# Layer 0 and layer 1: the engines' strip loops with four strips a turn in place of two

## Chip, cores and metric

The kernel runs on one core of a Trainium2 chip. The time is device microseconds (us) of one execution of the whole program; three runs of the kernel before took 21,091.03, 21,097.66 and 21,103.62 us. A core has TensorE (PE in the profile; PEld is its weight load), VectorE (DVE), ScalarE (ACT), GpSimd (POOL) and SyncE (SP). Each runs its own stream of instructions from memory, and they meet through semaphores. DMA queues carry data; among them are queues of the kind "instruction", which bring the engines their own programs.

## What is computed

Four images of 48 channels and 256 x 256 pixels go through six layers, each of them `x + layer(norm(x))`. The layers' kinds are in the name, `ccbcdd` being this program's letters; what the change touches are layer 0 and layer 1 (cut):

```
# layer 0
hidden = conv1x1(x, w_hidden);  qkv = depthwise3x3(hidden);  q, k, v = split(qkv, 3)
out = irfft2(rfft2(patches8x8(q)) * rfft2(patches8x8(k)))
normed = (out - mean_c(out)) / sqrt(var_c(out) + 1e-5) * gamma + beta
y = conv1x1(v * normed, w_out)
# layer 1
y = einsum(w_in, x);  y = irfft2(rfft2(patches8x8(y)) * fft_mask)
x1, x2 = split(depthwise3x3(y), 2);  y = einsum(w_out, gelu(x1) * x2)
```

Layer 2 samples an integral image of its input at four corners of a box for each pixel (a gather), and layer 3 is again a convolution, a gate and a patch transform.

## The kernel before

An image is worked in 32 strips of 8 rows. For each image in turn (`build`): layer 0 (for images 1 to 3 together with the box gather of the image before, `boxes`), then layer 1, the integral image, and the front of layer 2. The last box gather runs beside layer 3, which comes at the end for all images. So layer 0 and layer 1 run four times each, and each call has code of its own: the program holds four copies of either loop.

**Layer 0** (`layer0`, tag `a`) is a software pipeline with a step for every quarter strip of two rows, 128 steps an image. `pipeline` (L411) writes the steps of one engine: the first strip pair (8 steps) plainly, then a hardware loop over `u` (L421) with 8 steps a turn and 14 turns, then the last pair plainly and two steps that drain. PE, ACT and DVE each have their own loop of this shape. SP's loop over strip pairs (L486) and POOL's gather loop (L1828) are written apart. In a step PE makes the convolution for q and k of two rows (`conv_qk`, L530 and L533, into `p_qk`), the combination (L566), the convolution for v (L303 and L307, into `p_v`), the transforms of q and k (L547) and four transposes (L596). ACT begins a step with `gain` (L619), copies `p_qk` to `qk` (L614), takes two sums for the norm (L626, L633), and ends with `nrm` (L652) and `qh` (L661). DVE multiplies `t3` by `gain` (L701), and blends the gathered boxes in between (L1894, L1900). A loop's end therefore stands between L661 and L619 on ACT, and between L596 and L530 on PE.

**Layer 1** (`layer1`, tag `b`) is a pipeline with a step for every strip. Its `pipeline` (L822) has three plain steps, a loop with two steps a turn and 14 turns (L835), and five plain steps. A step has sixteen slots; PE's depthwise convolution is written as 16 small matmuls for each of 18 taps (L1010), so that a step of PE is some 1,600 instructions. A step begins on PE with `widen` (L966) and inverse transforms (L974), on ACT with the gelu of the strip before (L1129), on DVE with `weigh` (L1199) and `gates` (L1221). L1163 on ACT (the rows that strips share) runs once a step.

Semaphore targets are linear in the strip's number. Inside a loop they are computed from the loop's register, which costs an ALU instruction here and there.

Counted in the program as built, with matmuls and weight loads apart and register and wait instructions counted too, one turn of a loop is:

| loop | PE | ACT | DVE |
|---|---|---|---|
| layer 0, image 0 / images 1 to 3 | 1,045 / 1,081 | 323 | 202 / 222 |
| layer 1, image 0 / images 1 to 3 | 3,192 / 3,233 | 191 | 171 / 241 |
| layer 3, images 0 to 2 / image 3 | 2,342 / 2,260 | 181 | 378 to 380 / 238 |

Of the kernel before, what the change touches and what calls it, by code (L numbers as in the profile page):

```python
# [358 lines left out]
def layer0(env, src, dst, p, b, boxes=None, stats=None):  # L359
# [4 lines left out]
    U = S // 2  # L364
    C2, C6 = 2 * C, 6 * C
    with ExitStack() as ctx:
# [45 lines left out]
        def pipeline(eng, begin, step):  # L412

            n0 = b * (4 * S) + CREDIT
            begin(n0)
            for k in range(8):
                step(0, k, n0 + k, True, k >= 1, k >= 2, k >= 2 and k % 2 == 0)
            if U > 2:  # L420
                with eng.Fori(1, U - 1) as u:  # L421
                    for k in range(8):
                        step(u, k, n0 + u * 8 + k, True, True, True, k % 2 == 0)
            nl = n0 + 8 * U
            for k in range(8):
                step(U - 1, k, nl - 8 + k, True, True, True, k % 2 == 0)
            step(U, 8, nl, False, True, True, True)
            step(U, 9, nl + 1, False, False, True, False)
# [5 lines left out]
        with nc.Block() as block:  # L434
# [67 lines left out]
            def _(pe):  # L502
# [50 lines left out]
                def step(u, k, n, front, back, back2, turn_box):  # L553
# [35 lines left out]
                    if back:  # L589
# [5 lines left out]
                        for t in range(4):  # L595
                            m = pe.transpose(p_c[0:C2, 128 * t:128 * t + 128], nrm[:, t, :], env.c("ident"))  # L596
                            if beat and t == 0:
                                boxes.beat(m)
                        m.then_inc(turned_ready, 1)
                pipeline(pe, begin, step)  # L600

            @block.scalar
            def _(act):
# [5 lines left out]
                def step(u, k, n, front, back, back2, turn_box):  # L609
# [45 lines left out]
                    if front:  # L655
                        for h in range(2):
# [3 lines left out]
                            bank = p_f[0] if h == 0 else p_qk[0]  # L660
                            act.activation(qh[:, h, :, :].rearrange("p t c -> p (t c)"), bank[0:NPROD, 0:4 * C2], ACT.Copy).then_inc(qh_copied, 1)  # L661
                pipeline(act, lambda n0: None, step)

            @block.vector
            def _(dve):
# [29 lines left out]
                def step(u, k, n, front, back, back2, turn_box):  # L695
# [38 lines left out]
                    if front:  # L734
# [5 lines left out]
                        for h in range(2):  # L740
# [4 lines left out]
                            dve.tensor_tensor(prod[k % 2][:, h, :, :].rearrange("p t c -> p (t c)"), bank[0:NPROD, 0:4 * C2],  # L745
                                              qh[:, h, :, :].rearrange("p t c -> p (t c)"), ALU.mult).then_inc(prod_ready, 1)
                pipeline(dve, begin, step)


def layer1(env, src, dst, p, b, boxes=None):  # L750
# [6 lines left out]
    U = S // 2  # L757
# [23 lines left out]
    with ExitStack() as ctx:  # L781
# [43 lines left out]
        def pipeline(eng, begin, step):  # L825


            def half(u, k):
                return (U + u, k) if boxes else None
            n0 = b * S1 + 2  # L830
            begin(n0)
            step(n0, 0, True, False, False, False, None, True)
            step(n0 + 1, 1, True, True, False, False, half(0, 0), True)
            step(n0 + 2, 0, True, True, True, False, half(0, 1), True)
            with eng.Fori(0, U - 2) as u:  # L835
                step(n0 + u * 2 + 3, 1, True, True, True, True, half(u + 1, 0), True)
                step(n0 + u * 2 + 4, 0, True, True, True, True, half(u + 1, 1), True)
            step(n0 + S - 1, 1, True, True, True, True, half(U - 1, 0), True)
            step(n0 + S, 0, True, True, True, True, half(U - 1, 1), False)
            step(n0 + S + 1, 1, False, True, True, True, None, False)  # L840
            step(n0 + S + 2, 0, False, False, True, True, None, False)
            step(n0 + S + 3, 1, False, False, False, True, None, False)

        with nc.Block() as block:
# [86 lines left out]
            def _(pe):  # L931
# [91 lines left out]
                def step(n, par, front, mid, back, tail, half, more):  # L1023
                    m, o, l = n - 1, n - 2, n - 3
                    for t in range(NT):
# [55 lines left out]
                        if mid and t in CONV:  # L1081
                            taps(m, z[1 - par], *CONV[t], (2 if t in (3, 7, 10, 14) else 1) if half else 0)
                pipeline(pe, begin, step)

            @block.scalar
            def _(act):
# [50 lines left out]
                def step(n, par, front, mid, back, tail, half, more):  # L1137
                    m, o, l = n - 1, n - 2, n - 3
                    for t in range(NT):
# [29 lines left out]
                        if mid and t == 14:  # L1169
                            act.wait_ge(chain, (m + 1) * LINKS)  # L1170
                            act.wait_ge(y_ready, (m - 1) * NP)
                            act.activation(g_d[1 - par][HI], acc[0:64], ACT.Gelu).then_inc(gelu_ready, 1)
                pipeline(act, begin, step)

            @block.vector
            def _(dve):
# [46 lines left out]
                def step(n, par, front, mid, back, tail, half, more):  # L1223
                    m, o, l = n - 1, n - 2, n - 3
                    links = 0
                    for t in range(NT):
# [35 lines left out]
                        if mid and t == 15:  # L1262
                            dve.wait_ge(gelu_ready, m * 5 + 3)
                            dve.tensor_tensor(g_d[1 - par][HI], g_d[1 - par][HI], acc[HI], ALU.mult).then_inc(mul_ready, 1)
                pipeline(dve, begin, step)


# [1260 lines left out]
```

## Time and profile before

| | |
|---|---|
| median of three runs | 21,097.66 us |
| the profiled execution: its time / its span | 21,103.45 / 21,101.9 us |
| PE busy | 19,033.5 us (90% of the span) |
| DVE / ACT / POOL busy | 13,401.1 / 7,503.4 / 10,333.9 us |
| queue q8, instruction | 1,213 packets, 19.87 MB |
| queue q14, instruction | 570 packets, 4.67 MB |

The span runs from the first to the last instruction, 1.55 us less than the execution's own time. The four stretches of layer 0's loop lie near 376 to 1,736 us (image 0), 4,496 to 5,924, 8,733 to 10,170 and 12,986 to 14,324; those of layer 1's loop near 2,060 to 3,372, 6,245 to 7,600, 10,490 to 11,854 and 14,645 to 16,001. A wait that ends in "issue" is idle time in which the engine waited for nothing that the profile shows: no semaphore held it, it had no instruction to run. Branches and register instructions are not in the engines' rows.

### The profile page before, as it was taken

The page shows a single profiled execution, that of the slowest core. Times are in us where ns is not written, and L with a number is a line of the kernel's source. Part 1 is how long each engine was busy: PE and PEld are TensorE (multiplying, and loading weights), DVE is VectorE, ACT ScalarE, POOL GpSimd, SP SyncE. Part 2 cuts the span into 40 slices and gives each one's busy share as a digit, 9 for nine tenths or more (in the row PEclk, how much of TensorE's full clock was granted, in tenths as well). Part 3 has the DMA queues.
Part 4 walks back from the last instruction along what each step waited for, and adds up shares of the span by engine and source line. Part 5 has one row for each costly group of instructions (what it writes and reads, how often), then busy time and mean ns, then how long its engine had stood idle before and what let it go on. Part 6 is the DMA issues. An engine that isn't in the chain of part 4 may idle for free. (4 is left out here: it accounts for less than half of the span.)

```text
span 21101.9 us, 501412 instructions
## 1 busy us (share of the span) xinstructions
PE 19033.5 (90%) x172464; PEld 11794.6 (56%) x172464; DVE 13401.1 (64%) x22319; ACT 7503.4 (36%) x22720; POOL 10333.9 (49%) x8692
## 2 busy tenths in 40 slices
PE   6998998989989989899899898999998989898999
PEld 4665455456655554566555445665555456565666
DVE  4444445656667776666677766666777667777744
ACT  3554232145542221455422214663222122222222
POOL 0000000067767740677677406886774078787810
PEclk9999999999999999999999999999999999999999
DMA  3231112655533336455333364553434666666633
GB/s 92 68 70 45 35 36 84 140 112 113 113 99 111 110 119 145 109 112 113 99 110 111 112 151 111 121 121 100 111 110 126 134 146 150 149 149 146 147 88 78
DMA packets 932423, 2318.18 MB, mean 110 GB/s; under 512 B 276340, under 2 KB 528504, under 8 KB 844124
## 3 DMA queue, kind: packets, MB, share of 16 engines
q1 hardware_dynamic: 500560, 1364.68, 27.8%
q0 software_dynamic: 430080, 928.96, 16.7%
q8 instruction: 1213, 19.87, 0.4%
q14 instruction: 570, 4.67, 0.1%
HBM read 1915.53 MB, written 385.13 MB: 109 GB/s over the span
## 5 line engine op out<-in xcount | busy, mean ns | idle before, releaser
L1840 POOL DMA_INDIRECT e_got<-table,e_idx x6144 | 7479.2, 1217 | 2580.1 <-issue 1603.5
L1856 POOL DMA_INDIRECT e_got<-table,e_idx x2048 | 2553.1, 1247 | 691.6 <-issue 501.7
L1010 PE MATMUL b_p_conv<-b_z,b_diag 32*32 32x512 f32 x76032 | 2807.1, 599 | 3.3 <-issue 3.3
L530 PE MATMUL a_p_qk<-a_wst,a_stack 125*128 125x192 f32 x12288 | 2466.8, 337 | 230.9 <-ACT a_qh L661 214.0
L530 PEld LDWEIGHTS a_p_qk<-a_wst,a_stack 125*128 125x128 f32 x12288 | 2025.8, 191 | 670.5 <-issue 367.5
L1112 ACT ACTIVATE b_z<-b_p_z 128x256 f32<-128x256 f32 x2112 | 846.5, 401 | 4026.9 <-PE b_p_z L974 3608.2
L1894 DVE TENSOR_TENSOR e_got<-e_got,e_wt 128x1536 f32<-128x1536 f32 x1024 | 1778.6, 1752 | 684.9 <-DMA e_got<-table,e_idx 682.3
L1199 DVE TENSOR_TENSOR b_ym<-b_p_in,b_mask 128x512 f32<-128x512 f32 x1056 | 729.4, 691 | 1807.8 <-PE b_p_in L966 1807.6
L974 PEld LDWEIGHTS b_p_z<-const,b_ym 128*128 128x128 f32 x8448 | 1165.3, 198 | 1215.5 <-issue 713.3
L974 PE MATMUL b_p_z<-const,b_ym 128*128 128x128 f32 x8448 | 1541.1, 307 | 100.1 <-ACT b_z L1112 93.9
L2140 PE MATMUL d_p_v<-d_xs,d_ws 125*128 125x512 f32 x4608 | 1388.2, 449 | 64.0 <-issue 60.4
L1900 DVE TENSOR_TENSOR e_got<-e_got 128x1536 f32<-128x1536 f32 (+1 forms) x1024 | 1386.6, 1354 | 23.4
L303 PE MATMUL a_p_v<-a_xs,a_ws 125*96 125x512 f32 x4608 | 1363.1, 440 | 0.0
L1341 POOL DMA_DIRECT2D i_x<-planes x256 | 132.2, 516 | 2477.7 <-issue 1864.1
L1010 PEld LDWEIGHTS b_p_conv<-b_z,b_diag 32*32 32x32 f32 x76032 | 861.2, 103 | 732.2 <-issue 439.1
L2140 PEld LDWEIGHTS d_p_v<-d_xs,d_ws 125*128 125x128 f32 x4608 | 884.1, 201 | 341.2 <-issue 74.0
L303 PEld LDWEIGHTS a_p_v<-a_xs,a_ws 125*96 125x96 f32 x4608 | 747.9, 162 | 541.4 <-issue 284.9
L614 ACT ACTIVATE a_qk<-a_p_qk 128x384 f32<-128x384 f32 x1024 | 502.8, 491 | 1502.4 <-PE a_p_qk L533 1315.9
L966 PE MATMUL b_p_in<-b_w,b_xf 64*128 64x288 f32 x4224 | 847.8, 477 | 191.5 <-issue 172.4
L533 PE MATMUL a_p_qk<-a_wrs,a_rest 66*128 66x192 f32 x4096 | 1009.0, 327 | 0.0
L926 POOL MEMSET b_x<- 113x2064 f32 x4 | 7.3, 1818 | 2026.8 <-POOLq L243 2026.8
L547 PE MATMUL a_p_f<-a_qk,const 64*94 64x384 f32 x2048 | 821.7, 523 | 174.0 <-ACT a_qk L614 174.0
(291 smaller groups left out, 35444.6 us busy)
## 6 DMA issues: line engine op xcount, KB each, us to landing
e_got<-table,e_idx POOLq DMA_INDIRECT x8192
b_x<-planes SPq DMA_DIRECT2D x264, 395.1 KB
a_stack<-in_xp SPq DMA_DIRECT2D x256, 387.0 KB
c_stack<-planes SPq DMA_DIRECT2D x256, 387.0 KB
d_stack<-planes SPq DMA_DIRECT2D x512, 193.5 KB
table<-i_acc SPq DMA_DIRECT2D x256, 384.0 KB, 2.3
b_xr<-planes SPq DMA_DIRECT2D x264, 197.5 KB
planes<-b_out SPq DMA_DIRECT2D x264, 197.5 KB
```

Source lines behind the costliest of these rows:

```text
L303: mm = pe.matmul(out, ws[i][:, dx, lo:hi], xs[j][:, r0:r0 + QROWS, dx:dx + W], start=(dx == i == j == 0), stop=False)
L530: m = pe.matmul(dst_, st[:, row, dx + 128 * t:dx + 128 * t + 128], wst[:, dx, 0:2 * C2], start=(dx == 0), stop=False)
L533: m = pe.matmul(dst_, rt[:, row, 128 * t:128 * t + 128], wrs[:, 0:2 * C2], start=False, stop=True)
L966: pe.matmul(p_in[:, h, 0:NC], xf[k % 2][64 * h:64 * h + 64, :], w[64 * h:64 * h + 64, :], start=True, stop=True).then_inc(in_ready, 1)
L974: mm = pe.matmul(p_z[:, 128 * g:128 * g + 128], ym[k // 2 % 2][:, k % 2, 128 * g:128 * g + 128], env.c("idft"), start=True, stop=True)
L1010: mm = pe.matmul(p_conv[q // 2 * 2 + r % 2][BLK * c:BLK * (c + 1), :], diag[g][BLK * r:BLK * (r + 1), k, :], zs[BLK * r:BLK * (r + 1), g, ...
L1112: act.activation(zs[:, :, 2:2 + SROWS, 1 + 16 * k:17 + 16 * k], p_z[:, 0:NA].rearrange("p (g y x) -> p g y x", y=SROWS, x=16), ACT.Copy).t ...
L1840: pool.indirect_dma_start(out=self.got[q][:, t, c * REC:(c + 1) * REC], out_offset=None, in_=self.flat, in_offset=bass.IndirectOffsetOnAxi ...
L1856: pool.indirect_dma_start(out=self.got[q][:, t, c * REC:(c + 1) * REC], out_offset=None, in_=self.flat, in_offset=bass.IndirectOffsetOnAxi ...
L1894: dve.tensor_tensor(part, part, self.wt[i][:, at:at + 32].unsqueeze(2).broadcast_to([128, 32, C]), ALU.mult).then_inc(self.halved, 1)
L1900: dve.tensor_tensor(got[:, :, 0:half], got[:, :, 0:half], got[:, :, half:2 * half], ALU.add).then_inc(self.halved, 1)
L2140: mm = pe.matmul(out, ws[i][:, dx, lo:lo + 128], part(xs[j][:, :, dx:dx + W], side), start=(dx == k == 0), stop=False)
```

## The change

The loops of `pipeline` in layer 0 and layer 1 take twice the steps a turn and half the turns: 16 quarter-strip steps in place of 8, and four strips in place of two, seven turns each in place of fourteen. The plain steps ahead and behind are the same, and so are the steps themselves, their order and their semaphore targets, which are now computed from `v`. The loops of SP and POOL and those of the other layers are not touched.

```
-                with eng.Fori(1, U - 1) as u:
-                    for k in range(8):
-                        step(u, k, n0 + u * 8 + k, True, True, True, k % 2 == 0)
+                with eng.Fori(0, (U - 2) // 2) as v:
+                    for j in range(2):
+                        for k in range(8):
+                            step(v * 2 + (j + 1), k, n0 + v * 16 + (8 * j + k + 8), True, True, True, k % 2 == 0)
...
-            with eng.Fori(0, U - 2) as u:
-                step(n0 + u * 2 + 3, 1, True, True, True, True, half(u + 1, 0), True)
-                step(n0 + u * 2 + 4, 0, True, True, True, True, half(u + 1, 1), True)
+            with eng.Fori(0, (U - 2) // 2) as v:
+                for j in range(2):
+                    for k in range(2):
+                        step(n0 + v * 4 + (2 * j + k + 3), 1 - k, True, True, True, True, half(v * 2 + (j + 1), k), True)
```

In the program as built, a turn is then:

| loop | PE | ACT | DVE |
|---|---|---|---|
| layer 0, image 0 / images 1 to 3 | 2,088 / 2,160 | 643 | 399 / 438 |
| layer 1, image 0 / images 1 to 3 | 6,380 / 6,459 | 377 | 337 / 477 |

On ACT in layer 0 the eighth step of a turn was followed by the loop's branch, which goes back to the loop's first instruction; what stands behind it in the program is the code after the loop:

```order
L652 ACTIVATE a_nrm<-a_p_o,a_shift,a_rs 128x96 x4
L659 REGISTER_ALU
L661 ACTIVATE a_qh<-a_p_f 94x384
L661 ACTIVATE a_qh<-a_p_qk 94x384
L421 REGISTER_ALU
L421 COMPARE_AND_BRANCH
L619 ACTIVATE a_gain<-a_p_c,a_beta,a_gamma 96x512
```

Now the ninth step follows the eighth without a branch (line numbers are one higher):

```order
L653 ACTIVATE a_nrm<-a_p_o,a_shift,a_rs 128x96 x4
L660 REGISTER_ALU
L662 ACTIVATE a_qh<-a_p_f 94x384
L662 ACTIVATE a_qh<-a_p_qk 94x384
L620 ACTIVATE a_gain<-a_p_c,a_beta,a_gamma 96x512
L612 ISA
L615 ACTIVATE a_qk<-a_p_qk 128x384
```

The same pair of a register instruction and a branch now stands behind the sixteenth step. PE and DVE read alike, and in layer 1 the branch moves from behind each second strip to behind each fourth.

## Rows read from the trace of the kernel before

**Rows 1.** Waits that ended in "issue": total us, times, longest us.
```profile
PE b_p_in L966 <- issue: 172.4, 56, 4.1
ACT a_gain L619 <- issue: 160.9, 39, 4.9
ACT a_qk L614 <- issue: 156.2, 26, 8.5
ACT a_junk L626 <- issue: 93.0, 13, 7.7
...
DVE d_xs L321 <- issue: 22.5, 5, 6.2
```

**Rows 2.** DMA packets of layer 0's loop, image 1: queue, kind, packets, MB.
```profile
q14 instruction: 65, 0.53, 0.1%
```

**Rows 3.** The same of image 3's loop, all its queues.
```profile
q1 hardware_dynamic: 25670, 79.04, 30.2%
q0 software_dynamic: 39886, 81.73, 24.1%
```

**Rows 4.** The same of layer 1's loop, image 0; of a layer-3 turn, image 3.
```profile
q8 instruction: 182, 2.98, 1.0%
...
q8 instruction: 11, 0.18, 0.5%
```

**Rows 5.** Line L619, once a step: count, ns, first and last start (us).
```profile
L619 ACT ACTIVATE a_gain<-a_p_c,a_beta,a_gamma x6: 773/774/775, 409.4 to 472.5; 96x512 f32<-96x512 f32 x6
L619 ACT ACTIVATE a_gain<-a_p_c,a_beta,a_gamma x96: 772/774/777, 383.2 to 1617.6; 96x512 f32<-96x512 f32 x96
L619 ACT ACTIVATE a_gain<-a_p_c,a_beta,a_gamma x96: 772/773/776, 4503.4 to 5803.0; 96x512 f32<-96x512 f32 x96
L619 ACT ACTIVATE a_gain<-a_p_c,a_beta,a_gamma x96: 772/773/776, 8739.7 to 10047.1; 96x512 f32<-96x512 f32 x96
L619 ACT ACTIVATE a_gain<-a_p_c,a_beta,a_gamma x96: 772/773/776, 12988.5 to 14209.6; 96x512 f32<-96x512 f32 x96
```

**Rows 6.** Timeline at a loop end of layer 0, image 1: start, us, engine [idle before].
```profile
4717.63 1.24 PE L530 MATMUL a_p_qk<-a_wst,a_stack 125*128 125x192 f32 x6 [0.45 <-ACT a_qh L661]
...
4730.33 0.20 ACT L626 ACTIVATION_READ_ACCUMULATOR a_junk<-a_p_o 128x1 f32 x1 [6.94 <-issue]
...
4733.17 0.94 PE L547 MATMUL a_p_f<-a_qk,const 64*94 64x384 f32 x1 [4.97 <-ACT a_qk L614]
```

**Rows 7.** Line L1163, once a step of layer 1, as in rows 5.
```profile
L1163 ACT ACTIVATE b_z<-b_z x2: 1075/1075/1075, 3382.2 to 3428.3; 128x1032 f32<-128x1032 f32 x2
L1163 ACT ACTIVATE b_z<-b_z x26: 1074/1074/1076, 2125.2 to 3336.1; 128x1032 f32<-128x1032 f32 x26
L1163 ACT ACTIVATE b_z<-b_z x2: 1074/1074/1074, 6210.3 to 6257.9; 128x1032 f32<-128x1032 f32 x2
L1163 ACT ACTIVATE b_z<-b_z x26: 1074/1074/1077, 6310.6 to 7562.4; 128x1032 f32<-128x1032 f32 x26
L1163 ACT ACTIVATE b_z<-b_z x26: 1073/1074/1077, 10556.1 to 11816.6; 128x1032 f32<-128x1032 f32 x26
L1163 ACT ACTIVATE b_z<-b_z x26: 1073/1075/1077, 14710.3 to 15963.4; 128x1032 f32<-128x1032 f32 x26
```

**Rows 8.** Timeline at a loop end of layer 1, image 0.
```profile
2594.06 1.08 ACT L1129 ACTIVATE b_ga<-b_p_conv 128x512 f32<-128x512 f32 x2 [0.92 <-PE b_p_conv L1010]
2596.90 1.33 PE L966 MATMUL b_p_in<-b_w,b_xf 64*128 64x288 f32 x4 [3.11 <-issue]
...
2598.40 0.69 DVE L1199 TENSOR_TENSOR b_ym<-b_p_in,b_mask 128x512 f32<-128x512 f32 x1 [6.55 <-PE b_p_in L966]
...
2599.14 1.28 DVE L1221 TENSOR_TENSOR b_gate<-b_p_conv,b_ga 128x512 f32<-128x512 f32 x2
```

**Rows 9.** Windows around it: busy us (instructions) by engine, granted clock, DMA share, GB/s.
```profile
2575.00:2592.00 17.00, 17.00 (x315) 8.23 (x313) 6.87 (x15) 4.40 (x12) 0.00 (x0) 1.00 0.14 50
2597.00:2602.00 5.00, 5.00 (x12) 2.69 (x13) 2.02 (x4) 0.40 (x1) 0.00 (x0) 0.50 0.02 3
```

## Prediction

> **What bounds the kernel, and what a loop's end costs.** I read four views: the waits that end in "issue", the packets of the instruction queues, one line that runs once a step over each image's loop, and the timeline at a loop's end. PE sets the pace of both stages (17.00 us busy in a stretch of 17.00 [rows 9]), so what counts is what a loop's end does to PE. I call the jump from a loop's last instruction to its first a seam. A loop of 14 turns has 13, and the four images have 52 in each layer.
>
> In layer 0 it is ACT that pays. Its first instruction of a turn, L619, came late for want of an instruction 39 times, 4.1 us each: 13 seams of three images [rows 1]. A second stall of 6.0 to 7.2 us follows a few instructions later (26 + 13 times, on L614 or L626 [rows 1]). Image 1's loop fetched 65 packets from an instruction queue, five a seam [rows 2]; image 3's loop runs the same code and fetched none [rows 3]. ACT's loop of 323 instructions is thus sometimes kept whole and sometimes not, by where it happens to begin in memory. That makes image 3 a measurement of the same layer without seams: 95 steps took 1,221.1 us there, against 1,299.6 in image 1 and 1,307.4 in image 2 [rows 5]. Over the 11 whole seams in those stretches that is 78.5 / 11 = **7.1** and 86.3 / 11 = **7.9** us a seam. Image 0 has no boxes; its undisturbed step is 63.1 / 5 = 12.62 us, so 1,234.4 - 95 x 12.62 = 35.5, **3.2** us a seam [rows 5].
>
> In layer 1 it is PE that pays: 172.4 / 56 = 3.1 us before L966 [rows 1], 14 packets a seam (182 / 13 [rows 4]), since each turn of 3,192 instructions is fetched anew. Then PE runs at half its clock for a while (granted 0.50 behind the seam, 1.00 ahead of it, that is 1.2 in place of 2.4 GHz [rows 9]). An undisturbed step is 46.1 us in image 0 and 47.6 in image 1, for which two steps ahead of the loop stand [rows 7]. The 25 steps from the first to the last row hold 12 seams: (1,210.9 - 25 x 46.1) / 12 = **4.9**, and with 47.6 (1,251.8, 1,260.5 and 1,253.1 - 1,190) / 12 = **5.2, 5.9, 5.3** us.
>
> So seams cost today: layer 0, 13 x (3.2 + 7.1 + 7.9 + 0) = **237 us**; layer 1, 13 x (4.9 + 5.2 + 5.9 + 5.3) = **277 us**.
>
> **The change part by part.**
>
> Fewer seams: seven turns have 6, so 24 in place of 52 in each layer. No step, wait or order inside a turn changes, and the fewer branches and register instructions lie under PE's work.
>
> Layer 1, PE: still too long to be kept, the same price a seam. 6 x 21.3 = 128 us remain.
>
> Layer 1, ACT and DVE: their loops grow from 191 to 377 and from 171 or 241 to 337 or 477 instructions. Whether such a length is kept is seen from both sides: 323 both was and was not [rows 2, 3], 378 to 380 of DVE in layer 3 paid a stall of 22.5 / 5 = 4.5 us at its first instruction [rows 1]. I take DVE to miss in images 1 to 3 and leave ACT open. The cover is PE's own stall: DVE's L1199 waited 6.55 us, for PE and not for itself, and ACT's L1129 could start 2.84 us ahead of PE's L966 and is wanted by L1221 only at 2,599.14 [rows 8]: a delay of 4.1 us would move its end from 2,595.1 to 2,599.2, just there. I take 0.5 us a seam, with 0 and 3 as ends (ACT's second stall is not covered). Sum: 128 + 24 x 0.5 = **140 us**, so layer 1 gains 277 - 140 = **137 us** (range 277 - 128 - 72 = 77 to 149).
>
> Layer 0, ACT: 643 instructions, twice what misses in three images, so it misses in all four; image 3 now pays as images 1 and 2, 7.5 us. 6 x (3.2 + 7.1 + 7.9 + 7.5) = 154 us.
>
> Layer 0, PE: a new miss. A turn of 1,081 fetched nothing from q8 [rows 3], one of 2,260 in layer 3 fetched 11 packets [rows 4]. The new 2,088 and 2,160 lie close to the upper one, so I take it that they are fetched, at layer 1's 3.1 us of stall. In images with boxes this falls into a hole: PE's first matmul behind the seam waits for ACT's L661 anyhow, and later PE stands 4.97 us for ACT's L614 [rows 6]. What PE does late is taken from that hole. Image 0 has a smaller one (3.2 us of loss), so I add 1 us there. DVE's loop of 399 or 438 misses too, 4.5 us, while its next work, L701, waits for ACT's L619 (itself late by 4.1). I take 1 us a seam on every image for all this (0 and 3 as ends; below nothing is excluded, as no engine gets anything earlier). Sum: 154 + 24 x 1 = **178 us**, so layer 0 gains 237 - 178 = **59 us** (11 to 83; to 109 if image 3's ACT pays only 3.2).
>
> Fetching in the body: PE's loop in layer 0 now draws some 9 packets in 205 us. Layer 1 draws 14 in 97 us, and of the 56 waits before L966 that ended in "issue" 52 are its seams [rows 1]. I take nothing.
>
> Here the Trainium skill says something sharper. "Runtime: NRT & Kernel Launch", section "Instruction fetch mechanics", gives PE room for 2,048 instructions and the other engines for 512, filled in sequence, and says that a taken branch out of the window waits for a fetch. By its sizes PE's loop in layer 0, which fits today, falls out, which speaks against this change and is what the sum has taken from layer 3's row. By the same sizes ACT's loop of 323 fits wherever it begins and the new one of 643 does not; rows 2 and 3 contradict the first half. What would follow from the page there is rival E.
>
> Sum: 137 + 59 = **196 us**. The profiled execution took 21,103.45 us, which gives 20,907; it lies 5.8 us above the median of the three runs, so against the median **20,902 us**.
>
> **The rivals.**
>
> A. The forecast: 20,902 us. Its ends: all extras zero and image 3 cheap, 149 + 109 = 258 us, 20,840; extras of 3 us everywhere, 77 + 11 = 88 us, 21,010.
>
> B. PE's loop in layer 0 stays in place and no seam is dearer than today: 237 - 154 + 277 - 128 = 232 us, 20,866. For it: 2,088 and 2,160 are less than 2,260. Against it: the nearness.
>
> C. The stalls of one seam do not overlap but follow each other, because the three engines now ask for code at once while SP's loads and the gather use the same DMA engines. Then layer 0's seam takes 3.1 (PE) + 4.5 (DVE) = 7.6 us more: 6 x (25.7 + 30.4) = 337; layer 1's 4.1 (ACT) + 4.5 (DVE) = 8.6 more: 6 x (21.3 + 34.4) = 334. Together 671 against 514 us today: slower by 157, 21,255. For it: ACT's second stall is longer than the first [rows 1, 6]. Against it: the seams are nearly one point in time on all engines, and only the last to be ready counts. It decides from 24 x 2 seams dearer by (514 - 282) / 48 = 4.8 us each.
>
> D. PE starves inside the longer layer-0 body: at 0.75 us for each of some 9 packets x 28 turns the gain is gone, 21,098. Layer 1 shows no such stall.
>
> E. ACT's lost time in layer 0 is not the seam's and stays (237 us), and the longer loops of PE, ACT and DVE bring seams of their own on top, 178 us, against the 137 of layer 1: slower by 41, 21,139. The Trainium skill's sizes ("Runtime: NRT & Kernel Launch", "Instruction fetch mechanics") would have it so. Against it: image 3 loses nothing with the same code, and fetches nothing [rows 3, 5].
>
> **How the numbers follow.** A 0.78, B 0.10, C 0.05, D 0.04, E 0.03. The predicted time is A's. The range is A's ends, 20,840 to 21,010; it takes in B and leaves out C, D, E and a little of A, some 0.15. A measurement of this kernel tells about 0.2%, 42 us, from no change. Faster by more than that: A and B but for a little, 0.87; within: D, E and the rest of A, 0.08; slower: C, 0.05.
>
> **What would show it.** The waits for "issue" before L966 in layer 1 fall from 52 to about 24 with the same 3 to 4 us each; those of ACT at L619 from 39 to 24, now in image 3 as well. The q8 queue, absent from layer 0's loop, brings 9 or 10 packets a turn there; if it stays absent, B holds. In image 3's layer 0 the 95 steps get longer, by 5 or 6 seams of some 7.5 us, while those of images 1 and 2 get shorter by about as much. If seams in either layer take over 4.8 us more than today, C holds and the forecast is wrong.

## The result, and the profile after

The changed kernel takes **20,808.31 us** (median of 4 runs, 20,799.02 to 20,813.51) against 21,094.35 us beside it: ratio 0.9863, 95% interval 0.9848 to 0.9878. That is 286 us less, where 196 were forecast; the time lies 32 us below the range of 20,840 to 21,010. The direction was right, the size was not. Between the two profiled executions the difference is 297.5 us (spans 21,101.9 and 20,804.4 us).

The waits of the changed kernel that end in "issue" (total us, times, longest us) answer to [rows 1]; lines are one or two higher:

```profile
DVE a_t L702 <- issue: 97.4, 19, 6.5
ACT a_mu L631 <- issue: 86.5, 18, 6.6
PE b_p_in L968 <- issue: 79.2, 28, 3.9
ACT a_gain L620 <- issue: 73.4, 24, 4.1
...
DVE e_got L1896 <- issue: 49.2, 6, 8.6
PE a_p_qk L531 <- issue: 48.2, 25, 5.7
```

PE's stalls in layer 1 went from 56 to 28, ACT's at the head of a layer-0 turn from 39 to 24. New are PE's at L531, 25 of 1.9 us (before there was a single one): PE's layer-0 loop is fetched now. The packets of image 3's loop say the same, where [rows 3] had none (queue, kind, packets, MB, share of the 16 engines):

```profile
q8 instruction: 69, 1.13, 0.4%
q14 instruction: 76, 0.62, 0.2%
```

ACT's line that runs once a step of layer 0, over the whole of each image (first and last start, us):

```profile
L620 ACT ACTIVATE a_gain<-a_p_c,a_beta,a_gamma x128: 772/772/776, 198.0 to 1802.2; 96x512 f32<-96x512 f32 x128
L620 ACT ACTIVATE a_gain<-a_p_c,a_beta,a_gamma x128: 765/772/777, 4236.1 to 5933.0; 96x512 f32<-96x512 f32 x128
L620 ACT ACTIVATE a_gain<-a_p_c,a_beta,a_gamma x128: 765/772/775, 8411.1 to 10066.0; 96x512 f32<-96x512 f32 x128
L620 ACT ACTIVATE a_gain<-a_p_c,a_beta,a_gamma x128: 765/772/776, 12547.5 to 14196.6; 96x512 f32<-96x512 f32 x128
```

These are 1,604.2, 1,696.9, 1,654.9 and 1,649.1 us; the same line of the kernel before took 1,641.4, 1,721.8, 1,728.9 and 1,630.4. So layer 0 gained 117 us, twice the forecast's 59, and unevenly: 37, 25, 74 and -19.

And the line of layer 1 of [rows 7], over the same 26 steps:

```profile
L1165 ACT ACTIVATE b_z<-b_z x26: 1073/1076/1078, 2077.5 to 3260.3; 128x1032 f32<-128x1032 f32 x26
L1165 ACT ACTIVATE b_z<-b_z x26: 1072/1075/1077, 6204.9 to 7425.1; 128x1032 f32<-128x1032 f32 x26
L1165 ACT ACTIVATE b_z<-b_z x26: 1073/1075/1077, 10336.7 to 11561.5; 128x1032 f32<-128x1032 f32 x26
L1165 ACT ACTIVATE b_z<-b_z x26: 1074/1075/1077, 14468.5 to 15685.4; 128x1032 f32<-128x1032 f32 x26
```

With the forecast's steps of 46.1 and 47.6 us, (1,182.8 - 1,152.5) / 6 = 5.1 us a seam, and 5.0, 5.8 and 4.5: what the kernel before paid. Over all 32 rows of the line layer 1 gained 150 us. Some 30 us more lie outside both layers' loops, 17 of them in layer 3.

So the question for the runs is layer 0: a seam there costs 1.3, 11.2, 3.7 and 3.3 us in images 0 to 3 (worked out below), where the forecast had 4.2, 8.1, 8.9 and 8.5.

### The profile page after: what moved, and what is told of

Its sections match the earlier page's. It is cut to its first block and busy times, and to the rows that moved or that the text cites. A ratio compares the mean times of both kernels' runs of the same rounds, so it can differ in the third digit from the quotient of the medians.

```text
span 20804.4 us, 500656 instructions
## 1 busy us (share of the span) xinstructions
PE 18912.8 (91%) x172464; PEld 11734.2 (56%) x172464; DVE 13400.9 (64%) x22319; ACT 7497.1 (36%) x22720; POOL 10324.5 (50%) x8692
## 5 line engine op out<-in xcount | busy, mean ns | idle before, releaser
L531 PE MATMUL a_p_qk<-a_wst,a_stack 125*128 125x192 f32 x12288 | 2463.9, 337 | 273.0 <-ACT a_qh L662 212.3
L531 PEld LDWEIGHTS a_p_qk<-a_wst,a_stack 125*128 125x128 f32 x12288 | 2023.2, 191 | 709.0 <-issue 438.6
L723 DVE SCALAR_TENSOR_TENSOR a_out<-a_p_y,a_bo,a_out 49x512 f32<-49x512 f32 x512 | 377.4, 737 | 917.0 <-PE a_p_y L582 917.0
```

The source lines that it names most:

```text
L531: m = pe.matmul(dst_, st[:, row, dx + 128 * t:dx + 128 * t + 128], wst[:, dx, 0:2 * C2], start=(dx == 0), stop=False)
```

## The theory, and its rival

Two timelines of the changed kernel at a seam show where the difference lies: image 1, then image 2 (start, us, engine, in brackets the idle time before and what ended it).

```profile
4740.81 1.24 PE L531 MATMUL a_p_qk<-a_wst,a_stack 125*128 125x192 f32 x6 [1.91 <-issue]
4742.64 0.77 ACT L620 ACTIVATE a_gain<-a_p_c,a_beta,a_gamma 96x512 f32<-96x512 f32 x1 [3.35 <-issue]
4750.06 0.21 ACT L631 ACTIVATE a_mu<-a_total 128x4 f32<-128x4 f32 x1 [4.48 <-issue]
4753.38 3.43 DVE L1896 TENSOR_TENSOR e_got<-e_got,e_wt 128x1536 f32<-128x1536 f32 x2 [8.38 <-issue]
4759.22 1.40 ACT L653 ACTIVATE a_nrm<-a_p_o,a_shift,a_rs 128x96 f32<-128x96 f32 x4 [5.93 <-DVE a_shift L730]
4760.67 1.09 PE L597 MATMUL a_p_c<-const,a_nrm 128*96 128x128 f32 x4 [6.92 <-ACT a_nrm L653]
```

```profile
8698.31 1.24 PE L531 MATMUL a_p_qk<-a_wst,a_stack 125*128 125x192 f32 x6 [1.53 <-issue]
8699.87 0.77 ACT L620 ACTIVATE a_gain<-a_p_c,a_beta,a_gamma 96x512 f32<-96x512 f32 x1 [2.69 <-issue]
8703.42 0.69 DVE L702 TENSOR_TENSOR a_t<-a_p_v,a_gain 96x512 f32<-96x512 f32 x1 [5.58 <-issue]
8704.03 3.42 DVE L1896 TENSOR_TENSOR e_got<-e_got,e_wt 128x1536 f32<-128x1536 f32 x2
8707.43 0.21 ACT L631 ACTIVATE a_mu<-a_total 128x4 f32<-128x4 f32 x1 [4.35 <-issue]
```

In image 1 DVE runs four or five instructions, stands 8.4 us for its next packet, and hands the delay on: ACT's norm waits 5.9 us for DVE, PE 6.9 us for ACT. In image 2 DVE has its second stall nowhere near.

A packet of q14 is 8,192 bytes (4.67 MB / 570). The Trainium skill, "Runtime: NRT & Kernel Launch", section "Instruction fetch mechanics", counts 256 instructions to 16 KiB, so by an estimate from its figure such a packet is 128 instructions. The runs below agree, as the second stalls fall where this count puts them.

**Theory T.** The program of ACT and DVE comes in packets of 128 instructions with fixed borders. A loop of ACT or DVE that lies in three packets is kept; one that lies in four is fetched anew at each seam. Then the first packet ends the first stall, and the second comes several us later. What a seam costs depends on the *room*: the instructions from the loop's start to the end of its first packet, which are all that the engine can do until the second comes. The borders were fitted to which of ACT's loops in the kernel before are kept. Its rooms in layer 0 are then 25, 10, 4 (fetched) and 126 (kept); in the changed kernel 25, 16, 16, 16 on ACT and about 22, 4, 101, 70 on DVE.

**Rival P.** Each image has a price of its own, by its boxes and transfers, as the forecast took it.

## Experiments: one layer at a time

Layer 0's loops alone (the first hunk of the change):

> Layer 0's loops with four strips a turn, layer 1's as before. Theory T (what a seam costs depends on where the loop begins in the packets of 128 instructions that bring the programs of ACT and DVE: few instructions left in the first packet make a dear seam): the instructions left in the first packet are now 25, 74, 4 and 62 on ACT and 22, 42, 119 and 68 on DVE for images 0 to 3, so image 1 becomes cheap and image 2 dear; 6 x (1.4 + 3 + 6 + 3) = 80 us of seams in place of 237, about 20,940 us. Rival P (each image has a price of its own whatever the position, as the prediction had it): with the prices measured in the changed kernel (1.4, 11.1, 4.3, 3.1 a seam) 120 us remain, 20,977 us, with image 1 the dear one; with the prediction's own terms 178 us, 21,035 us.

Measured: 20,945.47 us (ratio 0.9925, 0.9908 to 0.9941). T's total of 20,940 and its order of images held: with the undisturbed lengths from the next section, a seam costs 2.0, 3.0, 5.1 and 2.7 us. Image 1, dear in the changed kernel, is cheap; image 2 is the dear one.

Layer 1's loops alone (the second hunk):

> Layer 1's loops with four strips a turn, layer 0's as before. Theory T: layer 1 gains about 150 us, and its longer code moves the layer-0 loops behind it, so that ACT's loop of 323 instructions now lies in three packets in images 1 and 3 (80 instructions left in the first) and in four in images 0 and 2 (25 and 16 left): image 1 loses its seams too, no stall of ACT at its loop's end there. 41 + 0 + about 85 + 0 us of seams in layer 0 in place of 237: 20,840 us in all. Rival P (a price for each image, whatever the position): layer 0 as before, 20,945 us.

Measured: 20,825.74 us (0.9872, 0.9855 to 0.9888), within 14 us of T and 119 us below P. Though nothing of layer 0 is edited, image 1 has no stall of ACT at its seams any more (1,639.5 us, of which 9.5 at other steps that I can't explain); image 3 has none, as before (1,630.9), and image 2 (room 16) still has. The two halves alone gain 152 and 272 us; together they gain 286. The parts don't add up because either moves the code of the other.

## Experiments: the room

Thirty instructions, once, in the kernel before:

```
+                for _ in range([30, 0, 0, 0][b]):
+                    act.sem_inc(turn, 1)
                 pipeline(act, lambda n0: None, step)
```

> The kernel before with 30 instructions more on ACT (semaphore increments that nobody waits for), once, ahead of layer 0 of image 0. Theory T: ACT's loop of 323 instructions then begins with 123, 108, 102 and 96 instructions left in its first packet, so it lies in three packets in all four images and is kept; no instruction packet and no stall at layer 0's seams, the 237 us go, 20,860 us. Rival P (what sets the loss is the image: its boxes, its transfers): no change, 21,095 us.

Measured: 20,861.37 us (0.9887, 0.987 to 0.9903). Thirty increments take 233 us off, T's 237 almost to the unit. Layer 0's line in that kernel, images 0 to 3:

```profile
L619 ACT ACTIVATE a_gain<-a_p_c,a_beta,a_gamma x128: 772/772/776, 203.9 to 1800.2; 96x512 f32<-96x512 f32 x128
L619 ACT ACTIVATE a_gain<-a_p_c,a_beta,a_gamma x128: 772/772/775, 4268.5 to 5898.5; 96x512 f32<-96x512 f32 x128
L619 ACT ACTIVATE a_gain<-a_p_c,a_beta,a_gamma x128: 772/772/775, 8416.1 to 10048.9; 96x512 f32<-96x512 f32 x128
L619 ACT ACTIVATE a_gain<-a_p_c,a_beta,a_gamma x128: 772/772/775, 12576.7 to 14206.0; 96x512 f32<-96x512 f32 x128
```

1,596.4, 1,630.0, 1,632.8 and 1,629.3 us: layer 0 without seams, the base for all prices here (a kernel's length less this, by its seams). Each length is of one profiled execution; where no seam costs anything, an image's length differs by up to 2.5 us between the kernels below, 0.4 us a seam of six, so smaller differences of prices tell nothing. The kernel before thus paid 45.0 / 13 = 3.5, 91.8 / 13 = 7.1, 96.1 / 13 = 7.4 and 0.1 us, as the forecast had read it. Queue q14 brought 375 packets in place of 570: 195 fewer, five for each of 39 seams.

The other way, less room in image 3 and other rooms elsewhere (93 increments ahead of image 0, 12 ahead of image 2):

```
+                for _ in range([93, 0, 12, 0][b]):
+                    act.sem_inc(turn, 1)
                 pipeline(act, lambda n0: None, step)
```

> The kernel before with 93 instructions more on ACT ahead of layer 0 of image 0 and 12 more ahead of image 2, so that ACT's loop begins with 60, 45, 27 and 21 instructions left in its first packet (25, 10, 4 and 126 in the kernel before) and lies in four packets in every image. Theory T (position sets the price): the loop is fetched in all four images, image 3 too, and the price falls with the room: image 0 about 1.5 us a seam (3.5 before), image 1 about 3 (7.1 before), image 2 about 5 (7.4 before), image 3 about 6 (0 before); 13 x 15.5 = 200 us in place of 237, 21,060 us. Rival P (each missing image has one price, about 7 us with boxes): 13 x (3.5 + 3 x 7.2) = 326 us, 21,185 us. Rival N (image 3 has no seams whatever the position): image 3 unchanged.

Measured: 20,998.06 us (0.9957, 0.9943 to 0.9971). P and N fall: q14 has 637 packets, 262 more than with all kept (260 are five for each of 52 seams), so ACT is fetched in all four images, image 3 too, and still the kernel is faster than before. Borders every 256 instructions, a loop being kept in two such blocks, fall as well: images 0 to 2 would have had rooms of 188, 173 and 155 here and been kept.

```profile
L619 ACT ACTIVATE a_gain<-a_p_c,a_beta,a_gamma x128: 772/772/776, 204.5 to 1800.9; 96x512 f32<-96x512 f32 x128
L619 ACT ACTIVATE a_gain<-a_p_c,a_beta,a_gamma x128: 772/772/777, 4263.5 to 5905.1; 96x512 f32<-96x512 f32 x128
L619 ACT ACTIVATE a_gain<-a_p_c,a_beta,a_gamma x128: 772/772/775, 8422.8 to 10107.9; 96x512 f32<-96x512 f32 x128
L619 ACT ACTIVATE a_gain<-a_p_c,a_beta,a_gamma x128: 772/772/775, 12634.7 to 14332.7; 96x512 f32<-96x512 f32 x128
```

Prices 0, 0.9, 4.0 and 5.3 us at rooms of 60, 45, 27 and 21: T's order, but 133 us in all where I had set 200; large rooms are cheaper than I thought. The two stalls of a seam in image 3 of this kernel:

```profile
13365.68 0.77 ACT L619 ACTIVATE a_gain<-a_p_c,a_beta,a_gamma 96x512 f32<-96x512 f32 x1 [4.14 <-issue]
13374.53 0.34 ACT L633 ACTIVATE a_junk<-a_p_o,a_mu 128x96 f32<-128x96 f32 x1 [5.77 <-issue]
```

The second comes behind the 21st instruction, as counted; in image 2 of the run with layer 1 alone it came behind the 16th. In the images with boxes it ends some 13.5 us behind the branch whatever the room (some 12 in image 0), so the room decides only how much ACT has done by then. The first stall of 4 us alone costs under 1 us. All prices with ACT alone missing in an image with boxes:

| room | kept | 74, 62 | 45 | 27 | 21 | 16 | 10 | 4 |
|---|---|---|---|---|---|---|---|---|
| us a seam | 0 | 0.7, 0.9 | 0.9 | 4.0 | 5.3 | 6.2 | 7.1 | 7.4, 7.1 |

Eight instructions on DVE in the changed kernel:

```
+                for _ in range([0, 8, 0, 0][b]):
+                    dve.sem_inc(turn, 1)
                 pipeline(dve, begin, step)
```

> The changed kernel with 8 instructions more on DVE, once, ahead of layer 0 of image 1. Theory T: DVE's loop of 438 instructions there begins with 125 instructions left in its first packet in place of 4 or 5, its second stall (8 to 9 us) goes, and image 1's loop loses about 26 us in place of 67: 41 us less than the changed kernel, 20,767 us. Images 2 and 3 stay within 10 us. Rival P: no change against the changed kernel, 20,808 us.

Measured: 20,780.77 us (0.9849, 0.9832 to 0.9865 against the kernel before). Image 1's line:

```profile
L620 ACT ACTIVATE a_gain<-a_p_c,a_beta,a_gamma x128: 766/773/777, 4239.6 to 5887.8; 96x512 f32<-96x512 f32 x128
```

1,648.1 us in place of 1,696.9: a seam there costs 3.0 us in place of 11.2. DVE's second stall is gone from that image. Its layer 0 gave 49 us; the whole only 28, where T had 41, as layer 3 and the program's start were 14 and 7 us longer in this profile.

## Experiments: which engine's miss costs what

`pipeline` of layer 0 got a parameter, so that each engine's loop can have two or four strips a turn on its own; layer 1 as before. PE alone (with the 30 increments of above, so ACT is kept), ACT alone, ACT and PE, ACT and DVE:

```
-        def pipeline(eng, begin, step):
+        def pipeline(eng, begin, step, pairs=1):
...
-                pipeline(pe, begin, step)
+                pipeline(pe, begin, step, 2)
```

> Layer 0 alone: PE's loop four strips a turn; ACT's and DVE's two strips a turn, with the 30 instructions ahead on ACT that keep its loop whole (as in e3). So of layer 0's loops only PE's is fetched anew. The same kernel without PE's longer loop took 20,861 us. Theory T (ACT sets the price, PE's stall of about 1.7 to 2.5 us is partly made up): 1 to 2 us a seam, 24 to 48 us more, 20,885 to 20,910 us. Rival Q (PE's own stall is all of the 3 us that the changed kernel pays where ACT has room): 3 us a seam, 72 us more, 20,933 us.

> Layer 0 alone: ACT's loop four strips a turn, PE's and DVE's two. ACT's loop begins where it does in the run with all of layer 0 changed (25, 74, 4 and 62 instructions left), and of the three engines only ACT misses. Theory T (ACT's first packets set the price, whatever the others do): image 1 and 3 about 3 us a seam, image 2 5.6 us as there, 80 us of seams in all, 20,940 us. Rival S (a seam is cheaper when PE and DVE miss with ACT, since the same room on ACT, 4, cost 7.4 us with ACT alone in the kernel before): image 2 pays 7.4 us, 47 us in six seams in place of 33.

> Layer 0 alone: the loops of ACT and PE four strips a turn, DVE's two. ACT begins with 25, 74, 4 and 62 instructions left in its first packet, as with ACT alone (3.3, 1.0, 7.1 and 1.0 us a seam) and as with all three (2.0, 3.0, 5.5 and 2.7). Theory V (it is DVE's fetch beside it that brings ACT's second packet sooner): image 2 pays 7 to 8 us a seam, images 1 and 3 2 to 3, as PE's own 1.7 is added. Theory W (it is PE's stall that makes image 2 cheaper): image 2 pays about 5.5 us.

> Layer 0 alone: the loops of ACT and DVE four strips a turn, PE's two. DVE begins with 22, 42, 119 and 68 instructions left. Theory V (DVE's fetch brings ACT's second packet sooner): image 2 pays about 5 us a seam, images 1 and 3 about 1 to 2. Theory W (PE's stall makes it cheaper): image 2 pays 7 to 8 us.

Measured: 20,928.54 us (0.9927, 0.991 to 0.9943), 20,929.11 (0.9926, 0.9909 to 0.9942), 20,965.20 (0.9935, 0.9916 to 0.9955) and 20,954.46 (0.993, 0.9911 to 0.995). By image, us a seam:

| missing | image 0 | image 1 | image 2 | image 3 |
|---|---|---|---|---|
| room on ACT (all but the first row) | 25 | 74 | 4 | 62 |
| PE | 1.6 | 1.8 | 1.2 | 1.2 |
| ACT | 3.3 | 0.7 | 7.1 | 0.9 |
| ACT and PE | 2.1 | 2.7 | 6.5 | 2.4 |
| ACT and DVE | 2.7 | 3.0 | 6.9 | 3.9 |
| all three | 2.0 | 3.0 | 5.1 | 2.7 |

PE's own price is T's 1 to 2 us. The total, 67 us above the kernel without PE's longer loop, is nearer to Q's, but only 34 of them lie in layer 0. Another 28 lie in layer 1 of image 3, whose loop isn't edited but stands elsewhere in PE's program (1,571.8 us over the 32 rows, 1,543.8 without PE's longer loop); that the place is what costs it there is argued. Where ACT has much room, images 1 and 3, the prices of ACT and PE nearly add (0.7 + 1.8 and 0.9 + 1.2 against 2.7 and 2.4). Where it has little, image 2, more misses make the seam *cheaper*, so S held against T there. Neither V nor W did: PE takes 0.6 us off, DVE alone nothing that can be told (0.2), and both together 2.0. The second stall of ACT in image 2 ends 13.4 us behind its branch with ACT alone, 13.2 with DVE, 12.4 with PE, 11.8 with all. Part of PE's share shows in the traces: SP waits for PE's convolution, and with PE missing as well its first load of `a_stack` was issued 2.2 us behind ACT's branch in place of 1.5 (means of image 2), and ACT's first instruction came 3.9 us behind it in place of 4.7. The rest is open.

T's room thus sets the price of a seam where ACT misses alone. With all three missing, and DVE not short of room, the seams with boxes cost 3.0 and 2.7 us at rooms of 74 and 62 on ACT, 2.9 to 3.7 at 16 (the changed kernel with and without the eight instructions on DVE), and 5.1 at 4.

## Experiments: why the second packet is late

The DMA share at a seam of image 1 in the kernel before (windows; busy us and instructions of PE, PEld, DVE, ACT, POOL, then granted clock, DMA share, GB/s):

```profile
4717.00:4721.00 4.00, 3.55 (x22) 2.78 (x20) 1.02 (x2) 0.58 (x2) 3.08 (x4) 1.00 1.08 155
4721.00:4725.00 4.00, 4.00 (x25) 3.40 (x23) 2.24 (x2) 1.52 (x5) 3.08 (x4) 1.00 1.02 150
4725.00:4729.00 4.00, 3.20 (x13) 1.79 (x11) 3.72 (x5) 0.00 (x0) 3.56 (x2) 1.00 0.99 211
4729.00:4733.00 4.00, 0.00 (x0) 0.00 (x0) 0.00 (x0) 2.61 (x16) 0.95 (x1) 1.00 0.97 218
4733.00:4737.00 4.00, 3.63 (x12) 1.55 (x12) 2.62 (x6) 3.38 (x11) 0.95 (x1) 0.58 0.15 50
```

For 16 us behind the seam the DMA engines are full (a share near 1). The largest transfers issued in that stretch are SP's (KB each):

```profile
a_stack<-in_xp SPq DMA_DIRECT2D x2, 387.0 KB
a_out<-in_xp SPq DMA_DIRECT2D x1, 387.0 KB
a_stack<-in_xp SPq DMA_DIRECT2D x1, 217.7 KB
```

They are transfers for the next strips, due at a strip's end, just where the loop's branch stands. ACT's loop was therefore begun two steps later, in the middle of a strip, with the same small rooms:

```
+            for k in range(late):
+                step(1, k, n0 + 8 + k, True, True, True, k % 2 == 0)
...
-                with eng.Fori(1, U - 1) as u:
-                    for k in range(8):
+                with eng.Fori(1, U - 1 - (late > 0)) as u:
+                    for k in range(late, 8 + late):
...
-                pipeline(act, lambda n0: None, step)
+                for _ in range([52, 80, 80, 62][b]):
+                    act.sem_inc(turn, 1)
+                pipeline(act, lambda n0: None, step, 2)
```

> The kernel before, with ACT's layer-0 loop begun two steps later (steps 2 to 7 of a strip pair and 0 and 1 of the next, 13 turns, 12 seams) and 52, 80, 80 and 62 instructions ahead, so that it begins with 25, 10, 4 and 16 instructions left in its first packet: 25, 10 and 4 as in the kernel before for images 0 to 2, and 16 as in image 2 of the run with layer 1 alone. What is new is the place of the seam: two steps behind the point at which SP's loads of the next strips keep the DMA engines full (share 0.97 to 1.08 for 16 us behind a seam of image 1 in the kernel before, 0.2 to 0.3 two steps later). Theory B (the second packet waits for those loads): it comes soon behind the first, the second stall shrinks to under 3 us, and the price falls to 1 to 2.5 us: 12 x 6 = 72 us of seams in place of 237, about 20,930 us. Theory F (the engine asks for its second packet about 9 us after the first whatever the DMA engines do): prices as at the same room before, 3.5, 7.1, 7.4 and 6.4 us: 12 x 24.4 = 293 us, about 21,150 us.

Measured: 20,874.59 us (0.9899, 0.9882 to 0.9916): B, and more than B; F falls. The lengths are 1,602.4, 1,635.3, 1,632.3 and 1,632.3 us, so 12 seams cost 0.5, 0.4, 0 and 0.3 us each at rooms of 25, 10, 4 and 16. ACT is fetched as before (q14: 626 packets, 251 above the kept kernel's 375), yet it stands less: 3.2 us in the mean at the first instruction of a turn (48 times, image 0 up to 6.3), and the second stall is short. DMA share and stalls at such a seam of image 2, room 4:

```profile
8744.00:8748.00 4.00, 3.55 (x22) 2.97 (x20) 1.02 (x2) 1.30 (x3) 3.09 (x4) 1.00 0.49 137
8748.00:8752.00 4.00, 4.00 (x26) 3.33 (x26) 3.63 (x3) 2.22 (x13) 3.70 (x2) 1.00 0.37 101
```

```profile
8747.56 0.77 ACT L627 ACTIVATE a_gain<-a_p_c,a_beta,a_gamma 96x512 f32<-96x512 f32 x1 [2.39 <-issue]
8750.05 0.49 ACT L622 ACTIVATE a_qk<-a_p_qk 128x384 f32<-128x384 f32 x1 [1.72 <-issue]
```

The second stall is 1.7 us; with ACT alone missing at the strip's end and the same room it was 8.1:

```profile
9578.46 0.77 ACT L624 ACTIVATE a_gain<-a_p_c,a_beta,a_gamma 96x512 f32<-96x512 f32 x1 [4.24 <-issue]
9587.37 0.49 ACT L619 ACTIVATE a_qk<-a_p_qk 128x384 f32<-128x384 f32 x1 [8.14 <-issue]
```

The packets' own records in the traces say it directly. In the kernel before, ACT's second packet began 8.9, 9.5 and 9.3 us behind the first (means over the seams of images 0 to 2); here it began 2.4, 2.6, 2.4 and 2.4 us behind it. Image 0, beside which no gather runs, is as late as the others, so the gather isn't needed for it. That the packet waits behind SP's transfers fits all this, but no run moved those transfers themselves.

The same with all three engines of the changed kernel (cut; the loop from step 18 on, six turns, with instructions ahead on ACT and DVE that leave them as little room as in the changed kernel):

```
+                for g in range(8, 18):
+                    step(g // 8, g % 8, n0 + g, True, True, True, g % 2 == 0)
+                with eng.Fori(0, (U - 4) // 2) as v:
+                    for g in range(18, 34):
+                        step(v * 2 + g // 8, g % 8, n0 + v * 16 + g, True, True, True, g % 2 == 0)
```

> The changed kernel with layer 0's loops of PE, ACT and DVE all begun later, two steps into a strip (six turns of 16 steps, five seams an image), and with instructions ahead on ACT (4, 32, 32, 32) and DVE (82, 83, 67, 67), so that they begin with as little room as in the changed kernel: 25, 16, 16, 16 left on ACT, and about 22, 5, 102, 72 on DVE. Theory B (what makes a layer-0 seam dear is that second packets wait behind SP's loads, on DVE too): all seams cost 1 to 2 us, image 1's too, 20 x 1.5 = 30 us in place of 117, about 20,720 us. Rival R (DVE's second packet in image 1 is late for another reason): image 1 keeps about 9 us a seam, 70 to 80 us of seams, about 20,765 us.

Measured: 20,799.91 us (0.9863, 0.9847 to 0.988), no gain that can be told from the changed kernel, where B expected some 90 us. By image the lengths of 1,617.3, 1,648.5, 1,656.2 and 1,649.6 us are 4.2, 3.7, 4.7 and 4.1 us for each of five seams. Image 1 fell from 11.2 to 3.7, so DVE's late packet there went with the place too, and R falls. But B missed as well: the other images did not get cheaper, and 83 us of seams remain in layer 0 where 30 were expected. PE's stall there is 59.6 / 20 = 3.0 us, longer than the changed kernel's 1.9; that it sets these prices is argued:

```profile
ACT b_ga L1138 <- issue: 82.3, 24, 4.9
ACT a_gain L623 <- issue: 68.6, 20, 6.1
PE a_p_qk L534 <- issue: 59.6, 20, 4.5
```

The first of these rows is new: the added instructions put ACT's layer-1 loop of 377 into four packets, and it misses at all 24 seams of layer 1. Over the four images layer 1 is 21 us longer than in the changed kernel, 0.9 us a seam. That is not ACT's price alone: the edit moves PE's loops too, beside which layer 1 of image 3 became 28 us longer in the run with PE alone, and image 0 got no longer (1,454.1 us over the 32 rows, 1,456.3 in the changed kernel) though ACT misses there as well.

## Experiments: a version that beats both

If a kept loop has no seams, layer 0 needs no longer turns, only ACT's room. Layer 0 as before with increments ahead, and layer 1 without a loop (28 strips written out, first with 30 ahead in image 0, then 55, 50, 59 and 59 in the four images and layer 3 written out as well) or with 14 strips in each of two turns (55, 15, 36 and 30 ahead):

```
-            with eng.Fori(0, U - 2) as u:
+            for u in range(U - 2):
...
-                with eng.Fori(0, TURNS) as v:
+                for v in range(TURNS):
```

```
+            M = 7
+            with eng.Fori(0, (U - 2) // M) as v:
+                for j in range(M):
+                    for k in range(2):
+                        step(n0 + v * (2 * M) + (2 * j + k + 3), 1 - k, True, True, True, True, half(v * M + (j + 1), k), True)
```

> A version that should beat both: layer 0's loops as before (two strips a turn, kept by PE and DVE), with the 30 instructions ahead on ACT that keep its loop too; layer 1 without a loop (28 strips written out on PE, ACT and DVE). Theory T: no seams in either layer; 237 + 277 = 514 us less than before, 20,580 us, if straight code is fetched ahead in time. Rival D (PE, ACT or DVE starve in straight code, as a packet is fetched anew for each strip): layer 1 gains nothing, about 20,860 us.

> Layer 1 without a loop, layer 0 as before. In the first such run the code of layer 1 had moved ACT's layer-0 loop to 45 and about 35 instructions left in images 1 and 3, and these paid 1.0 and 3.1 us a seam, 52 us. Here 55, 50, 59 and 59 instructions ahead bring it to about 98 left in every image. Layer 3 is written out too (four turns of six strips, where DVE stalled 4 to 6 us at the seams of three images). Theory T: the 52 us go, 20,615 us, and layer 3 gives 0 to 40 us: 20,575 to 20,615 us.

> Layer 0 as before, with instructions ahead on ACT (55, 15, 36 and 30 for images 0 to 3), so that its loop begins with 98 to 104 instructions left in its first packet in every image and is kept. Layer 1: 14 strips in each of two turns, so one seam an image. Theory T: layer 0 has no seams (237 us less), layer 1 keeps 21 of 277 us: 493 us less than before, 20,600 us; if straight code in layer 1 costs the 0.5 us a step that it cost without a loop, 42 us more, 20,642 us.

Measured: 20,667.72 us (0.9799, 0.9782 to 0.9815), 20,606.25 (0.9765, 0.9749 to 0.9781) and **20,585.95** (0.9755, 0.9738 to 0.9771). The last beats the changed kernel by 222 us and the kernel before, run beside it, by 515. Of PE's waits for an instruction before its first matmul of a layer-1 step 8 are left:

```profile
PE b_p_in L970 <- issue: 15.8, 8, 4.0
```

The first of the three fell short since the longer layer 1 had moved ACT's layer-0 loops again: images 1 and 3 had rooms of about 45 and 35 and lost 12.5 and 40 us. With the rooms set anew that went. Written out, a step of layer 1 in images 1 to 3 takes 48.0 us, in a loop 47.5, so that in layer 1 one seam beats none, by 14 us in all; the cause of that half us is not known.

## Why the forecast was wrong

- **The seam as the unit, and that it is a fetch**: right. Prices read as 3.2, 7.1, 7.9 and 0 us were 3.5, 7.1, 7.4 and 0.1 against a layer 0 without seams.
- **Layer 1, 137 us**: right in its main term, 150 measured. The price of a seam stayed (20.4 us for the four images, 21.3 before [rows 7]), and 24 remain. The 0.5 us for ACT and DVE, 12 us in all, was not paid: ACT's loop of 377 instructions lies in three packets and is kept, and DVE shows no wait for an instruction in layer 1. Where ACT's loop was not kept, the seams were 0.9 us dearer, with PE's code moved as well.
- **Layer 0, ACT, 154 us**: this step failed in its price. That "it misses in all four" was right, and so was image 3's loss. But 6 x (3.2 + 7.1 + 7.9 + 7.5) carried prices of one layout over to another, and the change itself altered the rooms, to 25, 16, 16 and 16. At the prices of ACT missing alone (3.3 at 25 in image 0, 6.2 at 16 with boxes) I estimate 6 x (3.3 + 3 x 6.2) = 131 us.
- **Layer 0, PE and DVE, 1 us a seam, "below nothing is excluded, as no engine gets anything earlier"**: this step failed, and by more. PE misses, as taken (the Trainium skill's "Runtime: NRT & Kernel Launch", "Instruction fetch mechanics", gives it 2,048 instructions; 2,088 and 2,160 were fetched, 1,081 not), but stalls 1.9 us, not 3.1, and costs 1.2 to 1.8 alone. With ACT short of room, the misses of PE and DVE took time off the seam in place of adding to it, and ACT did get its instructions earlier: the changed kernel with eight instructions ahead on DVE pays 6 x (1.3 + 3.0 + 2.9 + 3.4) = 64 us where ACT alone would pay the estimated 131. Why it is that much stays open. Against it stands DVE's miss in image 1, 8 us a seam by a room of four, outside the 0 to 3 that I allowed. Together: 178 us forecast, 6 x (1.3 + 11.2 + 3.7 + 3.3) = 117 measured. That image 1's dear seam made up for part of the miss was luck: without it the kernel took 20,780.77 us, further still from the forecast.
- **The rest**: some 30 us outside the two loops were not forecast. Layer 3's code is the same but stands elsewhere; thirteen other kernels with the same layer 3 took 4,193 to 4,213 us for it, against 4,216 before and 4,199 after. I leave the cause open.
- **Rival B** fell (q8's packets in image 3's loop), **D** too (no stall of that size in the body). **E** fell: ACT's loss in layer 0 was the seams', since it went with them. The same section of the Trainium skill gives ACT 512 instructions, by which size alone a loop of 323 fits wherever it begins, as E took it; but it puts them in two lines of 256, by which the place matters. Here 30 instructions ahead decided whether the loop was fetched. **C** named SP's loads on the same DMA engines, which the seam in mid-strip bears out as far as the place goes, and had the wrong consequence: the stalls of three engines overlap, and with little room on ACT they are together cheaper than ACT's alone (5.1 against 7.1), with much room dearer by 2 us.
- Image 3 [rows 2, 3] was read well: kept "by where it happens to begin in memory". The forecast knew this and still used a price that hangs on the same position as if it were a constant. The range was too narrow for a term that the layout moves between 0 and 11 us a seam.

## What to carry to other kernels

A loop that is fetched anew at its branch, on one engine alone, costs what this engine can't do until the *second* packet lands, so look at where its branch stands against the big loads and how far behind its start a packet ends, before making it longer. Where several engines are fetched anew at one point, don't add their prices: measure them together. Any edit to one stage moves the code of all later ones: count where each loop begins after the edit, and don't carry a stall's size over from the old layout. Where a loop nearly fits, a few dozen idle instructions ahead of it can be worth more than half the turns, and the branch can be moved to a quiet place in the work.

## What the hardware showed

- A loop of 323 instructions on ACT was kept in three packets of 8,192 bytes and fetched in four, five packets a seam. One of 377 showed no stall at its seams in three packets and one at each of 24 seams in four.
- ACT's second packet began 8.9 to 9.5 us behind the first with the seam at a strip's end (DMA share 0.97 to 1.08 at a seam of image 1), and 2.4 to 2.6 us behind it with the seam two steps later (0.37 to 0.49 at a seam of image 2). The second stalls there were up to 8.1 us, and 1.7.
- With a room of 4, three engines that miss at once lost less (5.1 us) than ACT alone (7.1); with rooms of 74 and 62 they lost more (3.0 and 2.7 against 0.7 and 0.9).
